# A pre-norm layer on one core: attention rows split as they lie and transposed by DMAs, own banks for scores and context, softmax first in VectorE's order

## What is computed

```
x = x + attn(layernorm(x))
    q, k, v = h @ w.T + b, each reshaped to (tokens, 32 heads, 32)
    scores = einsum('bshd,bstd->bsht', q, k) / sqrt(32)
    context = einsum('bsht,bstd->bshd', softmax(scores), v)
x = x + ffn(layernorm(x))
    dq = nf4_quant_dequant(w)        # blocks of 64, absmax scaling
    out = (silu(x @ dq1.T) * (x @ dq2.T)) @ dq3.T     # hidden width 2752
```

## Time and profile before

| what | value |
|---|---|
| median of three runs | 2158.37 us (2157.68 to 2159.42) |
| the profiled execution's own time | 2155.4 us |
| its span, first to last instruction | 2153.5 us |
| mean granted TensorE clock | 0.957 |
| busy: TensorE, VectorE, ScalarE, GpSimd | 1981.1, 1840.6, 1492.4, 1166.5 us |

### The profile page before, as it was taken

How to read it: one execution, slowest core, us unless ns; L and a number is a source line. 1 busy time by engine, 2 the same in 40 slices (tenths; PEclk the granted TensorE clock), 3 DMA queues, 4 the chain that set the end, 5 groups by cost and what they waited for, 6 DMA issues and landing times. The chain is left out here.

```text
span 2153.5 us, 30876 instructions
## 1 busy us (share of the span) xinstructions
PE 1981.1 (92%) x10272; PEld 1070.2 (50%) x10272; DVE 1840.6 (85%) x1847; ACT 1492.4 (69%) x1665; POOL 1166.5 (54%) x674
## 2 busy tenths in 40 slices
PE   4699999999987199999999999999999999999998
PEld 3377777777767044444444444444444444444442
DVE  8578888888879789898989989899898989989882
ACT  5424242424226688898989889798988979988782
POOL 0100101010111567878787777878778787786873
PEclk7799999999976599999999999999999999999999
DMA  7123434343323831121212212121212222212113
GB/s 283 58 75 114 143 110 132 112 143 110 122 70 103 311 68 47 42 56 41 57 44 54 58 39 58 39 58 39 58 39 51 47 49 49 58 39 54 35 35 156
DMA packets 219616, 175.24 MB, mean 81 GB/s; under 512 B 143664, under 2 KB 186672, under 8 KB 219568
## 3 DMA queue, kind: packets, MB, share of 16 engines
q1 hardware_dynamic: 217456, 166.23, 27.4%
q10 hardware_dynamic: 2112, 8.39, 1.0%
HBM read 115.34 MB, written 25.17 MB: 65 GB/s over the span
## 5 line engine op out<-in xcount | busy, mean ns | idle before, releaser
L1271 DVE SCALAR_TENSOR_TENSOR bank<-signs,bank 128x1024 f32<-128x1024 int8 (+2 forms) x792 | 964.3, 1218 | 99.6 <-ACT signs L1171 72.9
L1171 ACT ACTIVATE signs<-w_nat,compare_bias 128x1024 int8<-128x1024 f32 (+2 forms) x924 | 987.5, 1132 | 3.3 <-issue 2.5
L1402 PE MATMUL bank<-x2T_hi,w12T_hi 128*128 128x512 f16 x1376 | 523.2, 380 | 32.5 <-DMA w12T_lo<-half 25.0
L1403 PE MATMUL bank<-x2T_lo,w12T_hi 128*128 128x512 f16 x1376 | 523.0, 380 | 0.0
L1404 PE MATMUL bank<-x2T_hi,w12T_lo 128*128 128x512 f16 x1376 | 523.0, 380 | 0.0
L772 PE MATMUL bank<-wT_hi,xT_hi 128*128 128x512 f16 x768 | 296.6, 386 | 12.1 <-issue 12.1
L772 PE MATMUL bank<-wT_hi,xT_lo 128*128 128x512 f16 x768 | 296.7, 386 | 0.0
L1423 PE MATMUL bank<-w3T_hi,hT_hi 128*128 128x512 f16 x704 | 271.5, 386 | 23.2 <-DVE hidden L1279 19.6
L727 ACT ACTIVATE probs<-probs 128x1024 f32<-128x1024 f32 x16 | 16.9, 1058 | 376.1 <-DVE probs L653 376.1
L1425 PE MATMUL bank<-w3T_hi,hT_lo 128*128 128x512 f16 x704 | 270.4, 384 | 0.0
L1424 PE MATMUL bank<-w3T_lo,hT_hi 128*128 128x512 f16 x704 | 270.2, 384 | 0.0
(11 more groups left out here) (96 smaller groups left out, 2665.8 us busy)
## 6 DMA issues: line engine op xcount, KB each, us to landing
ff_raw<-in_L_ffn_w SPq DMA_DIRECT2D x63, 512.0 KB, 3.7
w_nat<-in_L_ffn_w SPq DMA_DIRECT2D x63, 512.0 KB, 3.8
x_nat<-in_L_attn_hidden_states SPq DMA_DIRECT2D x16, 512.0 KB, 3.9
x_res<-in_L_attn_hidden_states SPq DMA_DIRECT2D x16, 512.0 KB, 4.6
x<-x_res SPq DMA_DIRECT2D x16, 512.0 KB, 2.6
acc<-x ACTq DMA_DIRECT2D x4, 2048.0 KB, 20.5
out<-acc SPq DMA_DIRECT2D x16, 512.0 KB, 2.6
w_raw<-in_L_attn_wq SPq DMA_DIRECT2D x8, 512.0 KB, 6.9
```

The lines of the kernel that those rows point to most:

```text
L1171: nc.scalar.activation(signs[0:rows, ring(v, k), 0:cols], w_nat[0:rows, v % SLOTS, 0:cols], ACT.Sign, scale=COMPARE[SUMMED[k]][0], bias=co ...
L1271: V.scalar_tensor_tensor(to, part, HALF_STEP[SUMMED[k]], total, ALU.mult, ALU.add).then_inc(sign_used, 1)
L1402: nc.tensor.matmul(dst, hi, x2T_hi[:, toks, c], start=c == 0, stop=False)
L1403: nc.tensor.matmul(dst, hi, x2T_lo[:, toks, c], start=False, stop=False)
```

## The change

Five things.

1. The rows are split where they lie. ScalarE casts `x_nat` into `x_half[:, 0]` (`high_half`), GpSimd writes the rest into `x_half[:, 1]` (`low_half`); the factor `X_SCALE` is now in the reciprocal deviation. Two transposing DMAs that ScalarE issues (`turn_x`) bring them to `xT_hi` and `xT_lo`. TensorE's `turn` and both old splits are gone.
2. The same for `x_res` and `x2_half`, which are stored untransposed; `load_tokens` now transposes 512 rows from DRAM in each of its eight DMAs. The first waits for the last of ScalarE's transposes.
3. Scores keep banks 4 and 5, the context gets 6 and 7. The scores no longer wait for `ctx_read`, the context does. The scores lie between the seventh and the fourteenth matmul of the q projection.
4. VectorE's order: the row maximum and the subtraction come right after the first half of q and ahead of the normalization of `x_nat`; one look moves behind the reciprocal, the normalization of `x_res` behind the transposition of q. Pieces of the feed-forward program in steps 15 to 17 move with them.
5. `p_diag` is placed in two halves, eight instructions; the context's first 16 matmuls wait for the first only. `qkv` has two places instead of three.

SyncE's `x_res` load now stands behind all looks' loads and waits for GpSimd's low half; GpSimd's low half of `x_res` stands behind the feed-forward piece of its step.

```diff
-        def turn(rows, done):
-            for h in range(2):
-                for c in range(4 * h, 4 * h + 4):
-                    last = nc.tensor.transpose(bank[:, TURN + h, (c % 4) * P:(c % 4 + 1) * P], rows[:, c * P:(c + 1) * P], ident[:])
-                last.then_inc(done, 1)
-
-        def split_hi(act, n, hi, turned, hi_done):
-            for h in range(2):
-                act.wait_ge(turned, 2 * n + h + 1)
-                nc.scalar.activation(hi[:, 4 * h:4 * h + 4].rearrange("p c s -> p (c s)"), bank[:, TURN + h],
-                                     ACT.Copy, scale=X_SCALE).then_inc(hi_done, 1)
-
-        def split_lo(dve, n, lo, hi, hi_done, lo_done):
-            for h in range(2):
-                dve.wait_ge(hi_done, 2 * n + h + 1)
-                nc.vector.scalar_tensor_tensor(lo[:, 4 * h:4 * h + 4].rearrange("p c s -> p (c s)"), bank[:, TURN + h], X_SCALE,
-                                               hi[:, 4 * h:4 * h + 4].rearrange("p c s -> p (c s)"),
-                                               ALU.mult, ALU.subtract).then_inc(lo_done, 1)
+        def high_half(act, rows, half, done):
+            nc.scalar.activation(half[:, 0], rows, ACT.Copy).then_inc(done, 1)
+
+        def low_half(pool, rows, half, done):
+            nc.gpsimd.tensor_tensor(half[:, 1], rows, half[:, 0], ALU.subtract).then_inc(done, 1)
+
+        def turn_x(act, n, slot):
+            for i, (to, done) in enumerate(((xT_hi, x_hi_done), (xT_lo, x_lo_done))):
+                act.wait_ge(done, n + 1)
+                act.sem_inc(held, 1)
+                act.dma_start_transpose(to[:, slot], x_half[:, i]).then_inc(x_ready, 16)
...
-        mixing = bank[:, 4:6].rearrange("p b n -> p (b n)")
-        scores = mixing.rearrange("p (t h) -> p t h", h=HEADS)
-        context = mixing.rearrange("p (t d) -> p t d", d=HD)
+        scores = bank[:, 4:6].rearrange("p b n -> p (b n)").rearrange("p (t h) -> p t h", h=HEADS)
+        context = bank[:, 6:8].rearrange("p b n -> p (b n)").rearrange("p (t d) -> p t d", d=HD)
...
-                for look in todo[1:4]:
+                for look in todo[1:]:
                     load_ff(*look)
                 if end and attend:
-                    sp.wait_ge(x2_turned, 2 * (n - 1))
+                    sp.wait_ge(x2_lo_done, n - 1)
                     load_res(sp, n - 1)
-                for look in todo[4:]:
-                    load_ff(*look)
                 if end:
-                    sp.wait_ge(x2_lo_done, 2 * n)
+                    sp.wait_ge(x2_lo_done, n - 1)
                     sp.sem_inc(held, 1)
-                    for dram, part in ((x2_hi_dram, x2_hi), (x2_lo_dram, x2_lo)):
-                        sp.dma_start(dram[bass.ds((n - 2) * P, P), :], part[:].rearrange("p c s -> p (c s)")).then_inc(x2_out, 16)
+                    for i, dram in enumerate((x2_hi_dram, x2_lo_dram)):
+                        sp.dma_start(dram[bass.ds((n - 2) * P, P), :], x2_half[:, i]).then_inc(x2_out, 16)
...
                     nc.gpsimd.tensor_tensor(x_res[:], x_res[:], flipped[:], ALU.add).then_inc(res_done, 1)
+                if normalize:
+                    pool.wait_ge(x_hi_done, n + 2)
+                    low_half(pool, x_nat[:, 1 - u], x_half, x_lo_done)
+                if end:
                     pool.wait_ge(var2_ready, n - 1)
                     nc.gpsimd.tensor_tensor(rstd2[:], var_eps2[:], power[:, 0:1], ALU.pow).then_inc(rstd2_ready, 1)
                 if feed and attend:
                     next(feed)
+                if end:
+                    pool.wait_ge(x2_hi_done, n - 1)
+                    low_half(pool, x_res[:], x2_half, x2_lo_done)
...
+                if project:
+                    evacuate(n, u, it, 0, 0)
+                if attend:
+
+                    dve.wait_ge(scores_done, n)
+                    seq.mark(nc.vector.tensor_reduce(row_max[:], scores, AX.X, ALU.max))
+                    seq.wait(dve)
+                    nc.vector.tensor_tensor(probs[:], scores, row_max[:].unsqueeze(2).to_broadcast([P, QUAD, HEADS]),
+                                            ALU.subtract).then_inc(centered, 1)
+                    if feed and not project:
+                        next(feed)
...
                 if normalize:
-                    split_hi(act, n + 1, xT_hi[:, 1 - u], x_turned, x_hi_done)
+                    act.wait_ge(normed, n + 2)
+                    act.wait_ge(x_ready, 32 * (n + 1))
+                    high_half(act, x_nat[:, 1 - u], x_half, x_hi_done)
                 if attend:
                     act.wait_ge(p_ready, n)
                     if end:
                         act.wait_ge(context_done, n - 1)
-                    place(p_diag, flipped[:], p_placed)
+                    place(p_diag, flipped[:], p_placed, 2)
+                if normalize:
+                    if not (it is None and n == 0):
+                        act.wait_ge(projected, 6 * n)
+                        act.sem_inc(held, 1)
+                    turn_x(act, n + 1, 1 - u)
...
+                    if early:
+                        skip, slots = 6, skip
...
-                        pe.wait_ge(p_placed, n)
+                        pe.wait_ge(p_placed, 2 * n - 1)
                         pe.wait_ge(v_ready, n)
+                        if end:
+                            pe.wait_ge(ctx_read, n - 1)
                     for t in range(first, last):
+                        if t == QUAD // 2:
+                            pe.wait_ge(p_placed, 2 * n)
...
             def load_tokens(b):
-                tiles = slice(b * ST_BLOCK, (b + 1) * ST_BLOCK)
+                if b == 0:
+                    sp.wait_ge(g["x_ready"], 32 * T)
                 for part, dram in ((x2T_hi, x2_hi_dram), (x2T_lo, x2_lo_dram)):
-                    sp.dma_start(part[:, tiles].rearrange("p t c s -> p t (c s)"),
-                                 dram.rearrange("(t p) f -> p t f", p=P)[:, tiles]).then_inc(x2_in[b], 16)
+                    sp.dma_start_transpose(part[:, b], dram[b * BANK:(b + 1) * BANK, :]).then_inc(x2_in[b], 16)
```

143 lines of the change are left out of this document (59 added, 84 removed).

## The result

The changed kernel takes 2225.55 us (median of 5, 2213.99 to 2234.81) against 2158.37 us: ratio 1.031, 95% interval 1.027 to 1.035. It is 3.1% slower where 1.1% faster was forecast. The profiled execution took 2214.0 us, its span is 2212.2; before it was 2155.4 and 2153.5. It is the shortest of the five: the other four took 10 to 21 us longer, at a lower mean granted clock (0.918 to 0.926 against 0.930), so what follows explains 59 us of the median's 67.

A forecast was written before the change was run, and what follows sets the result against it. VectorE was taken to bound attention, TensorE the feed-forward part. Steps +39, last projected tile +7, seam -21 gave 25 us off 2155.4: 2130.4, plus 3.0 for the median 2133.4, said as 2134; range 2110 to 2172.

The forecast's parts named there:

- VectorE's own work: Attention step: low halves leave VectorE (2.4 us), the exponential's wait goes (0.4), x_nat normalizes quicker (0.4); 35.8 becomes 32.6, taken as 32.8.
- the looks keep their price: Attention step: VectorE's waits for ff_raw loads stay at 4.6 us on average, against 4.7 before.
- The second rival: Attention step: transposes among ff_raw loads hold the queue 3.0 us each, looks wait 3.0 us longer; 14 us slower, 2172; chance 0.10.
- ScalarE, placing, landing: Attention step: half placings take 4.6 us, transposes land 3.0 us after issue, at about 29 us, 4 us before TensorE wants them.
- Scores earlier in the projection are worth nothing by themselves: Attention step, query projection: moving the scores earlier was counted as no gain or loss, 0 us.
- worth nothing while VectorE ends last: Attention step: removing TensorE's two groups of transposes (1.09 and 1.07 us) was counted as no gain while VectorE is the bound.
- the third rival: Attention scores: thinner TensorE work among eight matmuls drops the clock to 0.50 every step, 42 us more, 2215; chance 0.08.
- the 2.01 us gap without a fall: Kernel before, attention step: TensorE's 2.01 us wait for xT_lo without a clock fall, cited against the clock falling.
- The opening: Start of the kernel: the halves and transposes add 0 to 2 us; taken as 0.
- The last projected tile: End of the projection: with own banks the first scores no longer wait for the context's read; 7 us won back.
- Between the stages: Seam from attention to feed-forward: token transposes from DRAM at 4.5 us a megabyte and later stores cost 21 us.
- fifth rival: Between attention and feed-forward: main sum with cheap token transposes, t = 2.8 us; gain 35 us, 2123; counted inside the main case's 0.46.

The follow-up runs named there:

- a_hold2: Changed kernel with one wait more: TensorE starts the keys' projection only when VectorE has normalized the next x_nat; 2197.8 us, ratio 1.019.
- a_noturn: Changed kernel with 28 of its 32 transposing DMAs from x_half replaced by copies of 16 bytes a partition; 2204.4 us, ratio 1.021.
- a_order_hold: a_order with one wait more: TensorE starts the values' projection only when VectorE has transposed the probabilities; 2164.0 us, ratio 1.005.
- b_early: Kernel before with one edit: scores stand among 8 matmuls of the query projection, matmuls 6 to 14; 2197.2 us, ratio 1.018.
- a_order: Changed kernel with VectorE's order and the scores' places as before; row split, transposing DMAs and own banks stay; 2227.1 us, ratio 1.033.
- a_fill16: Changed kernel with 16 extra matmuls on TensorE ahead of its wait for the keys, in front of the scores; 2196.9 us, ratio 1.018.
- a_hold: Changed kernel with one wait more: TensorE starts the keys' projection only when VectorE has read the second half of the queries; 2225.0 us.
- a_plain: Changed kernel with plain loads of the token halves in place of the eight 1 MB transposes from DRAM; 2223.4 us.
- a_wait: Changed kernel with the wait for the keys moved from inside the query projection to its start; ratio 1.032, from the two shorter of four runs.
- a_oh_seam: a_order_hold with token transposes moved: second block behind the last x2 store, third and fourth behind the second weight unit's transposes; 2163.5 us.
- a_thick: Changed kernel with 16 extra matmuls on a tile of zeros put between the scores, behind the wait for the keys; 2258.0 us, ratio 1.044.

## Why the prediction was wrong, by its own steps

**VectorE's own work: right. Its looks: a term mis-sized.** Without its waits VectorE's step shrank as forecast: `x_nat` normalizes in 0.80 us, the wait for the exponential is gone, and a step with four looks holds 27.4 us of other time (33.5 less 6.1 of waits) where before it held 30.6 (35.6 less 5.0). But "the looks keep their price" failed: forecast were 4.6 us of waits a step, measured 6.5 (68.8 us in 10.6 steps), 0.6 to 0.8 of it by the transposing DMAs. The second rival named that mechanism and gave it 3 us. The steps of 33.3 to 33.6 us hide this, for they all have four looks. Steps with five looks and no dip took 36.7 to 37.7 us in a_hold2, some waits for TensorE among them, and 35.9 in a_noturn. As an estimate, the forecast's 32.8 us with 1.9 more of waits is 34.7 us, and a_order_hold, which hardly dips, has 34.6. So of 3.0 us gained a step only some 1.2 were there even with the clock at 1.00: 16 us in 13 steps for 39.

**ScalarE, placing, landing: right in what counts.** Eight half placings took 5.1 us (4.6 taken). The transposes landed 5.0 to 5.3 us after issue, not 3.0, and TensorE never waited for `x_ready`.

**"Scores earlier in the projection are worth nothing by themselves", and TensorE's transposes go "worth nothing while VectorE ends last": the step that failed.** b_early shows what the first is worth: 39 us of loss. a_order shows that the second costs by itself too: with the scores spread as before, but without TensorE's transposes, it takes 2227.1 us, with dips in every other step (other parts of the change are in it too). The sum treated TensorE's 2 us of slack a step as harmless wherever it lies. The evidence used against the third rival was just this, "the 2.01 us gap without a fall", and it did not bear on the case: that gap stands in front of transposes and a dense projection. The change took the transposes away, so the same slack moved to the wait for the keys, in front of the thinnest work of the step. The third rival saw the dip but named thin work as its cause; a_fill16 and a_hold show thin work at 1.00 when no idle time is in front. It also had its frequency wrong (every step, 2215 us); every other step, plus a dearer place between the stages, made nearly the same time by other terms, so that its 2215 is near the measured time by luck. Twelve steps took 455.2 us against 431.0: 24 us lost where 36 were to be gained. As an estimate, twelve steps of 34.7 us would have taken 416, so the dips cost some 39 us in these twelve.

**The opening, 0 to 2 us forecast:** 6.0 us (the first normalization of a context at 150.2 instead of 144.2). What makes it was not tried.

**The last projected tile: failed.** The two steps behind these twelve took 85.6 us against 82.2, where 7 were to be won back; they hold dips of their own. In a_order_hold they took 73.1 us, 9 less than before, so the 7 us are there once the idle time is out of the way.

**Between the stages: nearly right.** VectorE waited 11.3 us for the `x1` store (10 and more forecast). Token transposes took 4.3 to 4.5 us each in the queue, the first 6.6 behind a weight load (t = 4.5 taken); a_plain, with plain loads in their place, won 6.3 us of stretch. By the rule of the Trainium skill ("Advanced Engine Details and Errata", section "X-Bar Transpose (TRN2)") that transposing DMAs are as fast as regular ones, t would have been 2.8 us, an estimate from the plain rate in the earlier trace rows; the measured 4.3 to 4.5 decide against it here. (The prediction gives its sum by that rule as 36 us and in its fifth rival as 35; its terms make 35.) From the last `x_res` to the issue of `acc` 15.4 us passed instead of 8.0 (5 forecast on top, 7.4 measured), from there to TensorE 34 instead of 30 (3.4 forecast). Not seen: more of VectorE's pieces of the feed-forward program stand between the softmax's subtraction and the transposition of the probabilities now (13.5 us from the start of the row maximum to it instead of 6.4), a loss of 7 us of which the earlier scores gave 3.4 back. Together that makes 27.4 for 21.

**What would have been the time with the clock at 1.00?** Not shown for the changed order itself. a_order_hold, the nearest, has steps of 34.6 and 2164 us: the attention part gains 19 us and the seam between the stages takes 25. So even then the 25 us of gain were not there; its steps are 1.8 us longer than the 32.8 forecast, with waits for looks of 5.3 us instead of 4.6.

## What to carry to other kernels

When a change takes work off an engine that is not the bound, ask where its new idle time will lie and what comes right behind it. On TensorE idle time in front of thin work (small float32 matmuls) halved the clock here for as long as the work stayed thin, while 1.6 to 2.1 us in front of transposes and a dense projection cost nothing more, and 4.1 us there a fall of 3 to 7 us. A wait put there on purpose can pay: one such line was worth 63 us here. It has to stand well ahead: six matmuls between it and the scores (a_wait) were not enough, and eight between it and the mixing let one long dip through in a_oh_seam. When a step alternates between two forms, compare like with like: here only the form with four looks looked like the forecast. And a totals comparison cannot resolve an edit of 10 us while dips come and go; compare stretches of one trace.

## What the runs showed of the hardware

A TensorE that the profile shows as busy throughout (12.00 of 12 us) ran at 0.50: eight scores took 1.75 us instead of 0.97. In the changed kernel the clock came back 3.0 to 4.5 us after the last of the scores (314.1 to 317.5 in the rows above), in a_hold 3 to 7 us after it fell. Idle times in front of scores in b_early, 200 to 600 us, that were followed by a dip: 0.48, 0.63, 0.74, 0.97 and 1.27 us; not followed by one: 0.42, 0.76, 0.95 and 1.05. In a_thick 1.35 and 1.39 us were, 1.02, 1.20 and 1.26 were not. So the length of one idle time does not decide it alone, and what else does stays open.

Adding 16 matmuls a step in front of the scores shortened the changed kernel by 1.3%, adding them between the scores lengthened it by 1.5%.

A 1 MB transpose from DRAM held its issuing queue for 4.3 to 4.5 us, as long as its data took (233 GB/s from 750 to 763 us), and for 24.9 us when ScalarE issued the 8 MB of `acc` in the same moment (782.5); everything behind it on SyncE waited that long. A plain load of 1 MB held it for 0.7 to 2.0 us at the same place in a_plain.
